# Two VectorE additions of a constant become operations with a constant tile, and the negated mean goes, in a three-layer graph-attention kernel

## What is computed

```python
for k in range(2):                                   # the two L layers
    q, kk = x @ Wq[k].T + bq[k], x @ Wk[k].T + bk[k]     # 128 features
    scores = where(adj == 0, -1e10, q @ kk.T / sqrt(128))
    attn = where(adj == 0, 0.0, softmax(scores))
    x = layer_norm(x + (attn @ x) @ Wc[k].T, ln_g[k], ln_b[k])
h = concat(softmax(where(adj == 0, -inf, q_h @ k_h.T / sqrt(32))) @ v_h for 8 heads)
y = h @ Wo + bo + x
out = (y - mean(y)) * rsqrt(var(y) + 1e-5) * gamma + beta
```

## Time and profile before

| | before |
|---|---|
| median of 3 runs | 1213.43 us (1211.64 to 1213.87) |
| profiled execution | 1213.54 us |
| its span in the trace | 1211.8 us |
| busy PE / VectorE / ScalarE / GpSimd | 95% / 82% / 76% / 44% of the span |
| granted TensorE clock, mean | 0.99 |

### The profile page before, as it was taken

The page is one execution under the profiler, slowest core; times in us unless marked ns, Lnnn a source line. Parts: engine busy times, 40 slices in busy tenths (PEclk is TensorE's granted clock), DMA queues, the critical chain, the costliest instruction groups (busy, mean ns, idle before and its releaser), DMA issues.

```text
span 1211.8 us, 28408 instructions
## 1 busy us (share of the span) xinstructions
PE 1155.4 (95%) x9572; PEld 840.7 (69%) x9572; DVE 989.3 (82%) x2680; ACT 923.2 (76%) x2112; POOL 538.9 (44%) x400
## 2 busy tenths in 40 slices
PE   5977999999999999999999999999999999999796
PEld 2754677777777777777777777777777777777463
DVE  4676789888888988888898888889888888988676
ACT  3235887878878787887878788787878888787774
POOL 1452344453464345346434534644453464444330
PEclk9799999999999999999999999999999999999999
DMA  8116161442615243251514325161442617132311
GB/s 242 36 36 153 23 176 36 124 90 71 153 36 167 45 122 88 67 161 36 172 39 123 89 81 146 36 177 34 125 91 78 145 37 179 32 76 79 95 33 36
DMA packets 170687, 114.06 MB, mean 94 GB/s; under 512 B 107184, under 2 KB 152240, under 8 KB 170544
## 3 DMA queue, kind: packets, MB, share of 16 engines
q1 hardware_dynamic: 168384, 104.37, 33.9%
q0 software_dynamic: 2160, 7.87, 1.9%
HBM read 61.87 MB, written 25.17 MB: 72 GB/s over the span
## 4 chain that ended last, share of the span: by engine, by line
PE 74%; DVE 11%; ACT 7%; issue 5%; DMA 2%; POOL 1%; DVEq 0%; POOLq 0%; SPq 0%; ACTq 0%
PE ps_j L793 32%; PE ps_t L806 18%; PE ps_j L910 9%; PE ps_s L779 6%; PE ps_s L785 6%; ACT probs L970 3%; ACT pt_l L976 2%; DVE some_l L1203 2%; DVE masked_s L1066 2%; DVE y_l L1217 2%; DMA xt<-ys 1%; PE ps_j L918 1%; DVE xw L1196 1%; DVE stats_L L1086 1%; DVE pt_l L1101 1%
## 5 line engine op out<-in xcount | busy, mean ns | idle before, releaser
L1066 DVE CUSTOM_DVE_ANT_0 masked_s<-ps_s,mask 128x512 f32<-128x512 f32 x640 | 424.4, 680 | 16.3 <-PE ps_s L785 14.5
L970 ACT ACTIVATE probs<-masked_s,nm_h 128x512 f32<-128x512 f32 x512 | 367.2, 718 | 88.6 <-DVE nm_h L1066 82.3
L806 PE MATMUL ps_t<-ident,probs 128*128 128x128 f32 x2560 | 391.4, 276 | 11.7 <-ACT pt_h L976 6.0
L806 PEld LDWEIGHTS ps_t<-ident,probs 128*128 128x128 f32 x2560 | 305.2, 142 | 93.9 <-issue 31.1
L976 ACT ACTIVATE pt_h<-ps_t 128x512 f32<-128x512 f32 x404 | 237.7, 588 | 64.5 <-PE ps_t L806 61.7
L785 PE MATMUL ps_s<-stack 128*128 128x512 f16 x512 | 194.7, 381 | 4.3 <-DVE nm_h L1066 3.8
L793 PE MATMUL ps_j<-xw,pt_l 128*128 128x256 f16 x1536 | 189.4, 275 | 0.0
L793 PEld LDWEIGHTS ps_j<-xw,pt_l 128*128 128x128 f16 x1536 | 151.4, 99 | 31.1 <-issue 0.5
L608 POOL TENSOR_TENSOR rstd_L<-var_eps_L,minus_half 128x4 f32<-128x4 f32 x32 | 32.8, 1025 | 264.8 <-DVE var_eps_L L1096 264.8
L910 PE MATMUL ps_j<-pt_h,v 128*32 128x256 f32 x2048 | 123.6, 382 | 2.2 <-DVE pt_h L1073 1.9
L1101 DVE TENSOR_TENSOR pt_l<-ps_t,pt_l 128x512 f16<-128x512 f32 x128 | 88.3, 690 | 37.6 <-ACT pt_l L976 28.4
(11 more groups left out here) (123 smaller groups left out, 1647.6 us busy)
## 6 DMA issues: line engine op xcount, KB each, us to landing
stack<-bounce SPq DMA_DIRECT2D x256, 128.0 KB, 3.1
bounce<-parts SPq DMA_DIRECT2D x64, 256.0 KB, 2.7
adj_t<-adj_dram SPq DMA_DIRECT2D x30, 512.0 KB, 5.4
x<-x_dram SPq DMA_DIRECT2D x16, 512.0 KB, 4.0
out_dram<-y_f POOLq DMA_DIRECT2D x15, 512.0 KB, 3.4
stack<-adj_dram SPq DMA_DIRECT2D x2, 512.0 KB, 5.6
pt_h<-l_wc SPq DMA_DIRECT2D x2, 256.0 KB, 4.3
xt<-ys SPq DMA_TRANSPOSE x32, 4.4
```

What stands on the lines that cost most here:

```text
L806: last = pe.transpose(ps_t[r % 2][:, t], probs[:, r, t * P:(t + 1) * P], ident[:])
L970: act.activation(probs[:, r], masked_s[:, r], ACT.Exp, bias=nm[:, n, r:r + 1], scale=-1.0, accum_out=total[:, n, r:r + 1]).then_inc(exps, 1)
L1066: dve.tensor_tensor_reduce(out=masked_s[:, r], in0=ps_s[scores_bank(pos)][:], in1=m[:, r], scale=-scale, scalar=NONE_LEFT, op0=ALU.add, op ...
```

## The change

The floor becomes `max` of `sum_l` with a tile `floor` that holds 0.5 everywhere, and the epsilon becomes an addition of `moments` and a tile `eps`; both were operations of one tensor with a constant in the instruction. The instruction that negates the mean is taken out, and the three places that added the negated mean subtract the mean itself, read from `moments` with a step of two elements. GpSimd fills the two tiles at its start, and VectorE waits for them once, ahead of its program. The two tiles take the room of the two that go.

```diff
-        minus_mean = {s: sb(f"minus_mean_{s}", [P, NT]) for s in "LF"}
+        floor = sb("floor", [P, NT])
+        eps = sb("eps", [P, NT])
...
             pool.memset(minus_half[:], -0.5).then_inc(half_in, 1)
+            pool.memset(floor[:], SUM_FLOOR).then_inc(floor_in, 1)
+            pool.memset(eps[:], LN_EPS).then_inc(floor_in, 1)
...
-                    last = pool.tensor_scalar(y_f[:, t], y_f[:, t], minus_mean["F"][:, t:t + 1],
-                                              rstd["F"][:, t:t + 1], ALU.add, ALU.mult)
+                    last = pool.tensor_scalar(y_f[:, t], y_f[:, t], moments["F"][:, t, 0:1],
+                                              rstd["F"][:, t:t + 1], ALU.subtract, ALU.mult)
...
-                    dve.tensor_scalar(minus_mean[s][:], moments[s][:, :, 0], -1.0, None, ALU.mult)
-                    dve.tensor_scalar(var_eps[s][:], moments[s][:, :, 1], LN_EPS, None, ALU.add)\
+                    dve.tensor_tensor(var_eps[s][:], moments[s][:, :, 1], eps[:], ALU.add)\
                         .then_inc(moments_ready[s], 1)
...
-                        last = dve.tensor_scalar(y_l[:, t], y_l[:, t], minus_mean["L"][:, t:t + 1],
-                                                 rstd["L"][:, t:t + 1], ALU.add, ALU.mult)
+                        last = dve.tensor_scalar(y_l[:, t], y_l[:, t], moments["L"][:, t, 0:1],
+                                                 rstd["L"][:, t:t + 1], ALU.subtract, ALU.mult)
...
-                        dve.tensor_scalar(some_l[:], sum_l[:, l_buffer(b, l)], SUM_FLOOR, None, ALU.max).then_inc(some_ready, 1)
+                        dve.tensor_tensor(some_l[:], sum_l[:, l_buffer(b, l)], floor[:], ALU.max).then_inc(some_ready, 1)
...
+            dve.wait_ge(floor_in, 2)
             program(walk)
...
-                dve.scalar_tensor_tensor(y_f[:, t], y_f[:, t], minus_mean["F"][:, t:t + 1], gain[:, 2],
-                                         ALU.add, ALU.mult).then_inc(normed["F"], 1)
+                dve.scalar_tensor_tensor(y_f[:, t], y_f[:, t], moments["F"][:, t, 0:1], gain[:, 2],
+                                         ALU.subtract, ALU.mult).then_inc(normed["F"], 1)
```

More of the change, by code:

```diff
@@ L221, in graph_attention @@
         weights_in = sem("weights_in")
-        ident_zero, ident_in, half_in = sem("ident_zero"), sem("ident_in"), sem("half_in")
+        ident_zero, ident_in, half_in, floor_in = sem("ident_zero"), sem("ident_in"), sem("half_in"), sem("floor_in")
         mean_in, bo_added, bx1_hi = sem("mean_in"), sem("bo_added"), sem("bx1_hi")
```

## The result

The changed kernel takes 1217.18 us, the kernel before 1213.57 us in the same comparison (medians of 10 runs each). The ratio is 1.0024, with a 95% interval of [1.0016, 1.0032]: slower by about 0.2 to 0.3%, where 1211.8 us had been forecast. The profiled execution took 1217.45 us, its span is 1215.7 us.

The account below looks back on a forecast made before the run. PE, busy for 95% of the span, was taken to lose 0.32 us per turn to VectorE's floor stalled by GpSimd. Savings of 1.2 + 0.5 = 1.7 us from 1213.54 gave 1211.8 us, with an 8 in 10 range of 1206.8 to 1213.9.

Parts of the forecast that it names:

- the subtraction of the mean takes the place of the addition: GpSimd's F norm and VectorE: as many instructions and elements as the addition, so no added cost on VectorE.
- the rival that says otherwise: GpSimd's subtraction in the F norm is dearer, over 0.2% slower from y = 80 on, up to 1223 us; chance 0.06.
- y: Extra ns for each of GpSimd's four F norm instructions; 204 from the nearest dear row, lengthening the gap by 4y - 95.
- the argument against: GpSimd's subtraction takes 2.13 us for 1024 elements, its addition 2.36, so subtracting is not the slower one.
- The stall stays: VectorE's floor, as two tensors, is still held by GpSimd's addition of the shift: 0 us gained; chance 0.76.
- the held L1113: VectorE instruction with two SBUF tensors, ending 0.27 us behind GpSimd's subtraction, held for 0.289 us; taken as evidence for the floor.
- The earlier `var_eps`: F norm without the negated mean: `var_eps` 0.095 us sooner, shrinking PE's gap each turn, 1.2 us in 13 turns.
- The price of the stall: PE's gap of 0.32 us in 13 turns, 4.2 us; with the tail and other `var_eps`, 5.7 us.
- the rival that it goes: The two-tensor floor isn't held by GpSimd's addition: 5.7 us less, 1207.8 us; chance 0.15.

## Why the prediction was wrong

**The step that failed** is the sentence that the subtraction of the mean takes the place of the addition "with as many instructions and as many elements", and the weight of 0.06 for the rival that says otherwise. I had seen that no row shows GpSimd's one-tensor form with a subtraction, and priced it by a bound (y = 204 ns at most). It is y = 664 ns. What misled me was the argument against: GpSimd's operations of two tensors with a subtraction are no slower than those with an addition. That says nothing about the one-tensor form with operands by column; here addition takes 553 ns for 256 columns, subtraction 1217. Why GpSimd takes longer for it stays open; the runs show only that the operation does it and the place of the operand doesn't.

**The sum of that rival was wrong too, the other way.** It let every nanosecond of GpSimd's chain reach PE: 4 x 664 - 95 would have been 2.6 us in each turn, and 33 us in all. Measured are 0.15 us per turn, and some 2 us in the tail, which it had not seen. The floor is not bound to the addition of the shift; it waits for whichever GpSimd instruction is running when it starts. With the chain 2.66 us later that is the multiplication by the gain, which began 0.5 us before, and the addition of the shift comes behind the floor. Such a wait is bounded by the length of one GpSimd instruction less its head start, and the timeline shows how near to that bound it is: 1.70 us before, 1.85 now, of 2.36.

**The stall stays** was right, for the reason given: the held L1113 foretold it. The floor alone as an operation of two tensors left the time where it was. (The prediction looked for it beside the addition of the shift; in the changed kernel it is the multiplication by the gain that holds it.) The Trainium skill's page "SBUF — State Buffer", section "Who interferes with whom", says so of operations with two SBUF inputs, and here the trace agrees (1.85 us in the changed kernel, 0.02 behind GpSimd's end). Among operations of one tensor the same section names those in a 2-port mode; here the form with its constant from a column is held, too (up to 1.96 us), and the single columns are not (144 ns).

**The earlier `var_eps`** was right in mechanism and near in size: 0.095 us per turn by the working, 0.08 us between the two kernels with the dear subtraction. Its sum of 1.2 us in 13 turns, and 1.7 us in all, was never seen by itself: the kernel with GpSimd's addition makes the negated mean for F again, so only 0.015 us of the 0.095 were left to it, and its time is no evidence for the sum. The 0.08 us are the only direct evidence.

**The price of the stall**, 5.7 us with the tail for the rival that it goes, was near: 6.1 us without the floor, 4.4 us with four columns that take 0.33 us. In the steady stretch, 13 turns of 70.24 us instead of 70.57 make 4.3 us, where 4.2 had been worked out.

**The account of the 3.6 us.** PE's longer gap is 2.0 us in 13 turns. Of these the profiles show a part as time: from the first `rstd_F` to the one where the tail begins it is 917.9 and 918.1 us in the two executions of the kernel before, and 919.3, 919.6 and 919.6 us in the three of the changed kernel, 1.2 to 1.7 us more, because single turns of either kernel take some tenths longer than the rest and the kernel before loses more by them. The tail's late `rstd_L` is worth 2.0 to 2.1 us where the clock's low stretch lies alike, and 0.6 to 0.7 us against the first profile of before, where it doesn't. Together that is 3.2 to 3.8 us at the like pattern, around the 3.6 measured. How often each pattern of the clock comes in the timed runs is not known, so how near the sum comes is in part luck.

## What to carry to other kernels

- Before an instruction changes its operation on GpSimd, find a row with that very form (one tensor or two, constant or column) and that operation. An addition of a negated value and a subtraction are the same arithmetic and here 553 against 1217 ns. Where no such row exists, the unknown cost deserves a run or a wide chance, not an argument from another form.
- A small VectorE instruction whose mean is far above its least time may be held by GpSimd, as the floor was here (820 against 165 ns), and it is busy in the profile, not waiting. Its end some 0.02 us behind the end of a GpSimd instruction is the sign. Ask first what PE loses (here 0.32 of each 1.5 us), and then change the form that is held: four single columns instead of one instruction of four gave 4.4 us.
- The wait of a VectorE instruction that meets a running GpSimd instruction was bounded by that one instruction here. Making GpSimd's chain longer or shorter moves which instruction is met, so the price doesn't follow the chain's length: 2.66 us more of chain cost 0.15 us a turn. Where an engine waits for what GpSimd makes, as for `rstd_L` in the tail, the length does count.

## What the runs showed of the hardware that I had not expected

- GpSimd's one-tensor form with two column operands, 128x256 float32: 553 ns for add then multiply, 1217 ns for subtract then multiply. The place of the operand makes no difference (556 ns).
- On VectorE, 128x4 float32 from SBUF to SBUF beside a running GpSimd instruction of two SBUF tensors: held to its end with a constant (up to 1.70 us), with a second tensor (some 1.69, and 1.85 in the changed kernel), and with a constant from a column (some 1.67, once 1.96). A single column (144 ns) and the reciprocal (178 ns for 4 elements, 248 for 16) are not held.
- The same program has a stretch of 3.4 us at 1.2 GHz between 85 and 95 us in some executions and not in others; of the two profiled executions of the kernel before, the one with it is 2.4 us later. A like stretch in the tail costs less where a wait for a transfer follows that it can use up.
